# The last stage's entry placed in the last steps of the second attention layer, with two weight sets, and the second batch's rows beside the first products

## The chip, the cores and the metric

One core of one Trainium2 chip runs the whole computation in one launch. The metric is the device time in microseconds (us), the median of several executions. The profiler records one execution; its times are us from the start of its span. The engines are TensorE (PE), VectorE (DVE), ScalarE (ACT), GpSimd (POOL) and SyncE (SP), which only issues transfers here.

## What is computed

A batch of 2 x 512 rows with 512 columns goes through four residual blocks. Each has the form below; only the last two matter here.

```python
x = x + _layernorm(_L1_attn_ref(_layernorm(x), Wq, bq, Wk, bk, Wv, bv, Wo, bo, gq, gk))
x = x + _layernorm(_L1_ffn_ref(_layernorm(x), w1, w3, w2, lora_A1, lora_B1, ...))

def _L1_ffn_ref(x, w1, w3, w2, ...):       # HID = 1376, rank R = 16, SCALING = 2
    h1 = _lora_linear(x, w1, lora_A1, lora_B1)   # x w1' + 2 (x A1') B1'
    h3 = _lora_linear(x, w3, lora_A3, lora_B3)
    return _lora_linear(jax.nn.silu(h1) * h3, w2, lora_A2, lora_B2)
```

The second attention layer has 32 heads of 128, a norm on queries and keys, and a softmax over 512 keys.

## The kernel before

Everything is float32, and each matrix product is made of three TensorE passes over an upper and a lower part of both operands (`product`, L80 to L85; `rest`, L88 to L90, makes a lower part as the full value less the upper one). So every operand needs an upper copy (mostly ScalarE) and a lower one (VectorE or GpSimd).

The 1024 rows are 8 row tiles of 128 (t = 0 to 7), tiles 0 to 3 are batch 0 and 4 to 7 batch 1. The running attention output stands in `acc`, the normed and turned input of a stage in `xT`, and the residual rows in device memory (`kept`).

**Second attention layer** (`paired_attention`). Eight passes over head groups, the middle ones in a hardware loop. A pass has 32 steps (`TILES`), one for each tile of scores; its slots are 8 pairs of head and batch, four steps each. Each engine runs the same list of steps in order, with semaphores between the engines. Work that lags is placed by step: a slot s starts at step 4s; its exchange of the probabilities' 32x32 blocks through the DMA queue (`move`) is issued at 4s + 4, 16 issues, after a write of the inverse row sums; the landed blocks are halved at 4s + 8 and 4s + 9; the product with the values (`pv`) is at 4s + 10; VectorE scales its result one step later (into one buffer, `scaled`), ScalarE and VectorE halve it (`output_hi`, `output_lo`), and output products (`project`) follow. In the last pass the list goes on to step 43 (`END1`): slot 6's product is at step 34, slot 7's at 38, the last output products at 41 and 42, and `add_rows` adds them to `acc`. Batch 0's last output products are at 33 and 34.

**Last stage** (`swiglu_phase`, a block of its own: its instructions start when all engines have left the one before). First an entry, by steps (`norm_steps`, `FIRST`): for each row tile the norm of the attention output (`ATTN`), GpSimd's residual add, the norm of the sum (`FFN_IN`), four transposes on TensorE (`turn`), an upper and a lower part into `xT`. The norm is one statistic, an aggregate and an epsilon on VectorE, a root on GpSimd (`root`), a bias on VectorE (`center`), the scaling on ScalarE (`scaled`). Beside it the weights: HID is 11 sets (o = 0 to 10) of three 128 x 512 pieces (w1, w3, w2). The low-rank factors are folded into each: TensorE makes their product in a `merge` bank (`prepare`), VectorE adds it to the raw piece (`whole`), ScalarE takes the upper part, GpSimd the lower. The factors need the side matrices (`side`) and a small tile for each set. Then n = 0 to 21 steps, o = 0 to 10 for batch 0 and again for batch 1: 24 matmuls for h1 and h3, the gate, and 12 matmuls (`down`) for the step before. In batch 0 set o + 2 is prepared in step o. `FIRST` ends with tile 3 turned, batch 1's norms having begun by then; the turns of tiles 4 to 7 (`LATER`) are in n = 0 and n = 1. SyncE loads everything in the order of its list; both halves of the summed rows are written back to `kept` ahead of set 3's third piece.

## Time and profile before

| | us |
|---|---|
| median of 3 runs | 2255.28 (2251.87 to 2255.32) |
| the profiled execution, its own time | 2258.43 |
| its span | 2256.4 |
| TensorE busy in the span | 2104.3 (93%) |
| VectorE, ScalarE, GpSimd busy | 1673.7, 1350.8, 1220.6 |

The mean granted TensorE clock is 0.969 of full speed. A busy share of a whole span is a mean over stages; for a change at one place the timeline around that place is what counts. In a timeline the bracket at the end of a row tells how long the engine was idle ahead of it and who ended that. A run of equal instructions is one row with its count.

### The profile page before, as it was taken

The numbers are of one execution on the slowest core, as the hardware profiler recorded it, in microseconds if no ns is written. First come the engines' busy times: TensorE is split into PE (matmuls) and PEld (weight loads), VectorE is DVE, ScalarE is ACT, GpSimd is POOL, SyncE is SP. The second block draws the span as 40 slices with busy tenths as digits, with TensorE's granted clock in tenths as the row PEclk, the third lists the DMA queues.
The fourth block names the chain that finished last, engine by engine and source line by source line (L and its number), as shares of the span: only waits on it lengthen the run. The fifth ranks groups of instructions, "written<-read, shape, count | busy, mean of one in ns | idle before, by whom it ended". The sixth has DMA issues, their size and how long they took to land. (4 is left out here: it accounts for less than half of the span.)

```text
span 2256.4 us, 38456 instructions
## 1 busy us (share of the span) xinstructions
PE 2104.3 (93%) x10535; PEld 1776.3 (79%) x10535; DVE 1673.7 (74%) x2974; ACT 1350.8 (60%) x3637; POOL 1220.6 (54%) x983
## 2 busy tenths in 40 slices
PE   6999999999999769999999999999999999847998
PEld 4788888888887657888888888888888888636886
DVE  6778888888788856888788787787887888853422
ACT  5777777777776445666656566565665656533321
POOL 3878778787795544545545454454644445233400
PEclk9999999999999979999999999999999999967999
DMA  2434443434445322434444344443444443443210
GB/s 81 125 104 128 105 116 107 123 92 127 102 109 145 94 80 61 122 102 121 109 113 105 98 117 110 108 112 95 116 114 103 107 105 93 101 121 104 64 52 24
DMA packets 165904, 231.96 MB, mean 103 GB/s; under 512 B 47281, under 2 KB 77137, under 8 KB 165745
## 3 DMA queue, kind: packets, MB, share of 16 engines
q1 hardware_dynamic: 165744, 229.97, 38.4%
q8 instruction: 83, 1.36, 0.3%
q14 instruction: 77, 0.62, 0.1%
HBM read 114.23 MB, written 6.55 MB: 54 GB/s over the span
## 5 line engine op out<-in xcount | busy, mean ns | idle before, releaser
L90 POOL TENSOR_TENSOR l_probsT_lo<-l_moved,l_probsT_hi 128x512 fp32r<-128x512 f32 (+2 forms) x256 | 281.1, 1103 | 314.3 <-ACT l_probsT_hi L620 286.5
L614 ACT ACTIVATE l_probs<-l_score,l_negtop 128x512 f32<-128x512 f32 x256 | 175.7, 686 | 376.1 <-DVE l_negtop L719 375.8
L90 DVE TENSOR_TENSOR l_probsT_lo<-l_moved,l_probsT_hi 128x512 fp32r<-128x512 f32 (+1 forms) x256 | 286.3, 1119 | 33.3 <-ACT l_probsT_hi L620 33.2
L719 DVE TENSOR_REDUCE l_negtop<-l_score 128x1 f32<-128x512 f32 x256 | 176.0, 687 | 91.9 <-PE l_score L85 90.0
L1487 ACT ACTIVATE l_probs<-l_score,l_negtop 128x128 f32<-128x128 f32 (+3 forms) x256 | 134.8, 526 | 178.5 <-DVE l_negtop L1599 177.1
L83 PE MATMUL l_score<-l_kT_lo,l_qT_hi 128*128 128x512 f32 (+3 forms) x512 | 191.5, 374 | 43.5 <-POOL l_qT_lo L90 18.7
L83 PE MATMUL l_out<-l_w_out_lo,l_oT_hi 128*128 128x512 f32 x512 | 209.6, 409 | 5.4 <-DVE l_oT_lo L745 2.8
L1599 DVE CUSTOM_DVE_ANT_0 l_score<-l_score,l_mask 128x128 f32<-128x128 f32 (+3 forms) x256 | 126.2, 493 | 110.0 <-PE l_score L85 108.9
L83 PE MATMUL l_general<-l_w_qk_lo,xT_hi 128*128 128x512 f32 x512 | 201.1, 393 | 1.7 <-PEq L1113 1.7
L85 PE MATMUL l_out<-l_w_out_hi,l_oT_hi 128*128 128x512 f32 x512 | 201.3, 393 | 0.0
L84 PE MATMUL l_out<-l_w_out_hi,l_oT_lo 128*128 128x512 f32 x512 | 201.2, 393 | 0.0
L85 PE MATMUL l_general<-l_w_qk_hi,xT_hi 128*128 128x512 f32 x512 | 201.1, 393 | 0.0
L84 PE MATMUL l_general<-l_w_qk_hi,xT_lo 128*128 128x512 f32 x512 | 201.0, 392 | 0.0
L83 PE MATMUL l_general<-l_probsT_lo,l_v_hi 128*128 128x512 f32 (+3 forms) x512 | 183.5, 358 | 16.1 <-POOL l_probsT_lo L90 10.9
L85 PE MATMUL l_general<-l_probsT_hi,l_v_hi 128*128 128x512 f32 (+3 forms) x512 | 186.1, 363 | 0.0
L84 PE MATMUL l_general<-l_probsT_hi,l_v_lo 128*128 128x512 f32 (+3 forms) x512 | 185.2, 362 | 0.0
L85 PE MATMUL l_score<-l_kT_hi,l_qT_hi 128*128 128x512 f32 (+3 forms) x512 | 183.8, 359 | 0.0
L84 PE MATMUL l_score<-l_kT_hi,l_qT_lo 128*128 128x512 f32 (+3 forms) x512 | 183.7, 359 | 0.0
L734 DVE STREAM_TRANSPOSE l_blocks<-l_probs 128x512 f32<-128x512 f32 x256 | 177.9, 695 | 0.0
L607 ACT ACTIVATE l_squares<-l_y 128x128 f32<-128x128 f32 x512 | 151.9, 299 | 24.5 <-DVE l_y L679 24.5
L90 POOL TENSOR_TENSOR l_w_qk_lo<-l_raw_qk,l_w_qk_hi 128x512 fp32r<-128x512 f32 x60 | 77.7, 1295 | 156.7 <-ACT l_w_qk_hi L584 156.7
L83 PEld LDWEIGHTS l_score<-l_kT_lo,l_qT_hi 128*128 128x128 f32 x512 | 97.3, 190 | 70.6 <-ACT l_probs L1487 20.3
(221 smaller groups left out, 6352.2 us busy)
## 6 DMA issues: line engine op xcount, KB each, us to landing
l_moved<-l_blocks SPq DMA_DIRECT2D x1024, 64.0 KB, 2.0
l_moved<-l_blocks SPq DMA_DIRECT2D x512, 80.0 KB, 2.1
l_inv_all<-inv_rows SPq DMA_DIRECT2D x32, 512.0 KB, 4.4
l_raw_out<-l_wo SPq DMA_DIRECT2D x64, 256.0 KB, 4.5
l_inv_all<-inv_rows SPq DMA_DIRECT2D x64, 256.0 KB, 3.7
ffn_w_lo_words<-f_w SPq DMA_DIRECT2D x33, 256.0 KB, 2.8
l_raw_q<-l_wq SPq DMA_DIRECT2D x32, 256.0 KB, 4.3
l_raw_qk<-l_wq SPq DMA_DIRECT2D x64, 128.0 KB, 2.9
```

What stands on the lines that cost most here:

```text
L83: nc.tensor.matmul(out, left.hi, right.lo, start=first, stop=False, skip_group_check=True)
L84: nc.tensor.matmul(out, left.lo, right.hi, start=False, stop=False, skip_group_check=True)
L85: return nc.tensor.matmul(out, left.hi, right.hi, start=False, stop=last, skip_group_check=True)
L90: return engine.tensor_tensor(out, full, hi.bitcast(F32), ALU.subtract)
L607: last = act.activation(squares[:, h], y[:, b, t, h * HD:(h + 1) * HD], ACT.Square, accum_out=sumsq[:, b, j:j + 1])
L614: act.activation(probs[:, n % NPR], score[n % 2][:], ACT.Exp, bias=negtop[:, n:n + 1], accum_out=total[:, n:n + 1]).then_inc(s_exp, 1)
L719: dve.tensor_reduce(negtop[:, n:n + 1], score[n % 2][:], AXX, ALU.max, negate=True)\
L734: dve.transpose(to, probs[:, n % NPR]).then_inc(s_block, 1)
L1487: act.activation(probs[:, n % NPR, 0:width[t]], score[n % 2][:, 0:width[t]], ACT.Exp, bias=negtop[:, n:n + 1], scale=-1.0, accum_out=total ...
L1599: dve.tensor_tensor_reduce(out=score[n % 2][:, 0:w], in0=score[n % 2][:, 0:w], in1=mask[:, S - w:S], scale=-SCALE, scalar=3.0e38, op0=ALU. ...
```

## The change

A new class `Entry` holds the last stage's entry, its buffers, banks and semaphores. They are laid over the attention's memory: the attention's `y`, `qT`, `kT` and value weights move to the front of its memory, so that what is read latest lies behind what the entry writes. In the attention's last pass each engine gets work in steps 33 to 40, always after what stands in that step already:

- SyncE: the rows of batch 0 and the side matrices at step 22, tiles and pieces of sets 0 and 1 at step 26 (it waits for the slot 7 keys to be out of the transposed rows), the rows of batch 1 at step 33.
- step 33: side matrices and two tiles, upper and lower. Step 34: norms of the attention output of tiles 0 to 3. Step 35: their residual adds. Step 37: the input norms; step 38: their scalings, now into `acc`. Turns on TensorE at 38 (three) and 40; their upper parts at 39 and 40, lower parts at 39 and 40.
- the six merges at steps 34 to 36, the adds at 34, 35 and 37, upper parts at 37 and 38, lower parts at 38 and 39.

In the last stage step n = 0 starts at once. Batch 1's attention norms are at n = 0, the adds on GpSimd at n = 0 and 1, input norms at n = 1 and 2, scalings at 2 and 3, and one tile is turned at the end of each of n = 3 to 6, into a merge bank; sets from 2 on are prepared as before, but the third piece of set 2 at n = 1 ahead of set 3. The summed rows are written back ahead of set 9.

```diff
-END1 = TILES + REST_AT
...
+class Entry:
+    R3 = 96
+    PLACE = [0, 1, 9, 10, 7, 8, 2, 3, 4, 5, 6]
+    NEAR, NEAR2 = 5, 2
+    ROWS_AT, WEIGHTS_AT, MORE_ROWS_AT = 22, 26, 33
+    SIDE_AT, ATTN_AT, ADD_AT = 33, 34, 35
+    MERGE, WHOLE = {34: (0, 1), 35: (2, 3), 36: (4, 5)}, {34: (0, 1), 35: (2, 3), 37: (4, 5)}
+    WHOLE_HI, WHOLE_LO = {37: (0, 1, 2, 3), 38: (4, 5)}, {38: (0, 1, 2, 3), 39: (4, 5)}
+    FFN_IN, SCALE = [TB * (n,) for n in (37, 38)]
+    TURN, UPPER, LOWER = (38, 38, 38, 40), (39, 39, 39, 40), (39, 39, 40, 40)
+    STEPS = range(SIDE_AT, 41)
+    END = TILES + REST_AT
...
+        with ExitStack() as room:
+            self.near, self.near_words = self.tile_and_words(p, room, "ffn_w13_near", [P, self.NEAR, 4, 512])
+            self.tile_raw = p.sb(room, "ffn_tile_raw", [self.R3, 2, 3 * P])
+            self.w2_near, self.w2_near_words = self.tile_and_words(p, room, "ffn_w2_near", [P, self.NEAR2, 2, 512])
+            self.side = p.sb(room, "ffn_side", [self.R3, 3, D], F32R)
+            self.tile = p.sb(room, "ffn_tile", [self.R3, 2, 3 * P], F32R)
+            self.norms = RowNorms(p, room, ctx0, "ffn_norm", 3, half)
+            self.w2_far, self.w2_far_words = self.tile_and_words(p, room, "ffn_w2_far", [P, HT - self.NEAR2, 2, 512])
+            self.far, self.far_words = self.tile_and_words(p, room, "ffn_w13_far", [P, HT - self.NEAR, 4, 512])
+            self.merge, self.h, self.rows = (p.banks(room, n, k) for n, k in (("ffn_merge", 2), ("ffn_h", 2), ("ffn_rows", TB)))
...
+        self.x = self.near_words[:, 2:4].rearrange("p a b s -> p (a b) s")
+        self.side_raw = self.near_words[0:self.R3, 4, 0:3]
...
+    def turned(self, t):
+        return self.rows[t % (TB - 1)] if t < TB else self.merge[(3 * (t + 1) + 3) % 2]
+
...
+    def load_rows(self, sp, b):
+        rows = slice(b * TB, (b + 1) * TB)
+        sp.dma_start(self.x[:, rows], self.kept[:, rows]).then_inc(self.s_x[b], 16)
+
+    def load_side(self, sp):
+        for j, n in enumerate(("f_a1", "f_a3", "f_b2")):
+            sp.dma_start(self.side_raw[:, j], self.a[n]).then_inc(self.s_side, 16)
+
+    def load_weights(self, sp):
+        for o in range(2):
+            sp.dma_start(self.tile_raw[:, o], self.a["f_tile"][o]).then_inc(self.s_tile[o], 16)
+            for j in range(3):
+                sp.dma_start(self.raw(j, o), self.a[("f_w1", "f_w3", "f_w2")[j]][o]).then_inc(self.s_raw[j][o], 16)
+
+    def prepare(self, pe, o, parts=range(3)):
+        side, merge = self.side, self.merge
+        pe.wait_ge(self.s_tile_lo, o + 2)
+        for j in parts:
+            k = 3 * o + j
+            if k >= 2:
+                pe.wait_ge(self.s_whole, k - 1)
+            if j == 0 and TB + 2 <= o < TT + 2:
+                pe.wait_ge(self.s_x_lo, o - 1)
+            low = self.tile[:, o % 2, j * P:(j + 1) * P]
+            if j < 2:
+                for c in range(C):
+                    last = pe.matmul(merge[k % 2][:, c * P:(c + 1) * P], side[:, j, c * P:(c + 1) * P], low,
+                                     start=True, stop=True, skip_group_check=True)
+            else:
+                last = pe.matmul(merge[k % 2][:], low, side[:, j], start=True, stop=True)
+            last.then_inc(self.s_merged, 1)
+
+    def turn(self, pe, t):
+        pe.wait_ge(self.norms.normed[FFN_IN], t + 1)
+        if t == TB - 1:
+            pe.wait_ge(self.s_x_lo, 1)
+        if t >= TB:
+            pe.wait_ge(self.s_whole, 3 * (t + 1) + 2)
+        for c in range(C):
+            last = pe.transpose(self.turned(t)[:, c * P:(c + 1) * P], self.acc[:, t, c * P:(c + 1) * P], self.ident[:])
+        last.then_inc(self.s_turn, 1)
+
+    def tensor(self, pe, n):
+        for t, at in enumerate(self.TURN):
+            if n == at:
+                self.turn(pe, t)
+        for k in self.MERGE.get(n, ()):
+            self.prepare(pe, k // 3, (k % 3,))
+
...
+    def scalar(self, act, n):
+        if n == self.SIDE_AT:
+            act.wait_ge(self.s_side, 48)
+            act.activation(self.side[:], self.side_raw, ACT.Copy, scale=2.0).then_inc(self.s_tile_hi, 1)
+            self.tile_hi(act, 0)
+            self.tile_hi(act, 1)
+        if n == self.ATTN_AT:
+            self.scale_attn(act, range(TB))
+        for t in range(TB):
+            if n == self.SCALE[t]:
+                self.scale(act, t)
+        for t in range(TB):
+            if n == self.UPPER[t]:
+                self.upper(act, t)
+        for k in self.WHOLE_HI.get(n, ()):
+            self.whole_hi(act, k // 3, (k % 3,))
+
+    def scale_attn(self, act, tiles):
+        for t in tiles:
+            self.norms.scaled(act, ATTN1, t, self.acc[:, t], self.acc[:, t])
+
+    def upper(self, act, t):
+        act.wait_ge(self.s_turn, t + 1)
+        act.activation(self.xT.hi[:, :, self.cols(t)], self.by_chunk(self.turned(t)), ACT.Copy).then_inc(self.s_x_hi, 1)
+
+    def scale(self, act, t):
+        self.norms.scaled(act, FFN_IN, t, self.acc[:, t], self.x[:, t])
+
+    def scalar_second(self, act, n):
+
+        if TB <= n < TT:
+            self.upper(act, n)
+        if n == 0:
+            self.scale_attn(act, range(TB, TT))
+        for t in self.pair(n - 2):
+            self.scale(act, t)
+
+    def pair(self, k):
+        return range(TB + 2 * k, TB + 2 * k + 2) if 0 <= k < TB // 2 else []
+
...
+    def sums(self, dve, t):
+        dve.wait_ge(self.s_add, t + 1)
+        self.norms.sums(dve, FFN_IN, t, self.x[:, t])
+        self.norms.spread(dve, (FFN_IN, t))
+
+    def norm_attn(self, dve, tiles):
+        for t in tiles:
+            self.norms.sums(dve, ATTN1, t, self.acc[:, t])
+            self.norms.spread(dve, (ATTN1, t))
+            if t > tiles[0]:
+                self.norms.center(dve, ATTN1, t - 1)
+        self.norms.center(dve, ATTN1, tiles[-1])
+
+    def vector(self, dve, n):
+        if n == self.SIDE_AT:
+            dve.wait_ge(self.s_tile_hi, 1)
+            dve.scalar_tensor_tensor(self.side[32:64], self.side_raw[32:64], 2.0, self.side[32:64].bitcast(F32),
+                                     ALU.mult, ALU.subtract).then_inc(self.s_tile_lo, 1)
+            self.tile_lo(dve, 0)
+            self.tile_lo(dve, 1)
+        if n == self.ATTN_AT:
+            self.norm_attn(dve, range(TB))
+        tiles = [t for t in range(TB) if n == self.FFN_IN[t]]
+        for t in tiles:
+            self.sums(dve, t)
+        for t in tiles:
+            self.norms.center(dve, FFN_IN, t)
+        for t in range(TB):
+            if n == self.LOWER[t]:
+                self.lower(dve, t)
+        for k in self.WHOLE.get(n, ()):
+            self.whole(dve, k // 3, (k % 3,))
+
+    def vector_second(self, dve, n):
+        if TB <= n < TT:
+            self.lower(dve, n)
+        if n == 0:
+            self.norm_attn(dve, range(TB, TT))
+        for t in self.pair(n - 1):
+            self.sums(dve, t)
+        for t in self.pair(n - 2):
+            self.norms.center(dve, FFN_IN, t)
+
+    def add(self, pool, t):
+        pool.wait_ge(self.s_x[t // TB], 16)
+        pool.wait_ge(self.norms.normed[ATTN1], t + 1)
+        pool.tensor_tensor(self.x[:, t], self.x[:, t], self.acc[:, t], ALU.add).then_inc(self.s_add, 1)
+
+    def gpsimd(self, pool, n):
+        if n == self.ATTN_AT:
+            for t in range(TB):
+                self.norms.root(pool, ATTN1, t)
+        if n == self.ADD_AT:
+            for t in range(TB):
+                self.add(pool, t)
+        for t in range(TB):
+            if n == self.FFN_IN[t]:
+                self.norms.root(pool, FFN_IN, t)
+        for k in self.WHOLE_LO.get(n, ()):
+            self.whole_lo(pool, k // 3, (k % 3,))
+
+    def gpsimd_second(self, pool, n):
+        if n == 0:
+            for t in range(TB, TT):
+                self.norms.root(pool, ATTN1, t)
+        for t in self.pair(n):
+            self.add(pool, t)
+        for t in self.pair(n - 1):
+            self.norms.root(pool, FFN_IN, t)
+
+
...
+        y = sb("y", [P, B, TB, 512])
+        qT = split("qT", [P, 2, S])
+        kT = split("kT", [P, 2, S])
+        with ExitStack() as early:
+            raw_v = p.sb(early, "l1_raw_v", [P, C, HW])
+        w_v_lo = sb("w_v_lo", [P, C, HW], F32R)
+        w_v = Split(sb("w_v_hi", [P, C, HW], F32R), w_v_lo)
...
+                    if m.last and n == Entry.ROWS_AT:
+                        sp.wait_ge(s_free, m.done(USES1, ("y", 1, 1, TB - 1)))
+                        entry.load_rows(sp, 0)
+                        entry.load_side(sp)
+                    if m.last and n == Entry.WEIGHTS_AT:
+                        sp.wait_ge(s_free, m.done(USES1, ("tk", SLOTS - 1)))
+                        entry.load_weights(sp)
+                    if m.last and n == Entry.MORE_ROWS_AT:
+                        entry.load_rows(sp, 1)
...
+                    if m.last and n in Entry.STEPS:
+                        if n == Entry.TURN[0]:
+                            pe.wait_ge(s_free, m.done(USES1, ("pv", SLOTS - 2)))
...
+                    if m.last and n in Entry.STEPS:
+                        if n == Entry.ATTN_AT:
+                            dve.wait_ge(s_added, m.done(OUTS1, (1, 0, TB - 1)))
+                        entry.vector(dve, n)
...
@@ -1806,24 +2044,17 @@
                 sp.wait_ge(s_add, (b + 1) * TB)
                 sp.dma_start(batch(kept, b), batch(x, b)).then_inc(s_kept, 16)
 
-            sp.dma_start(batch(x, 0), batch(kept, 0)).then_inc(s_x[0], 16)
-            for o in range(HT):
-                if o == 0:
-                    for j, n in enumerate(("f_a1", "f_a3", "f_b2")):
-                        sp.dma_start(side_raw[:, j], a[n]).then_inc(s_side, 16)
-                if o >= 2:
-                    sp.wait_ge(s_tile_lo, o)
-                sp.dma_start(tile_raw[:, o % 2], a["f_tile"][o]).then_inc(s_tile[o % 2], 16)
-                if o == 1:
-                    sp.dma_start(batch(x, 1), batch(kept, 1)).then_inc(s_x[1], 16)
+            for o in range(2, HT):
+                if o == 9:
+                    sp.wait_ge(norms.normed[FFN_IN], TT)
+                    keep(0)
+                    keep(1)
+                    sp.wait_ge(s_kept, B * 16)
+                sp.wait_ge(entry.s_tile_lo, o)
+                sp.dma_start(entry.tile_raw[:, o % 2], a["f_tile"][o]).then_inc(entry.s_tile[o % 2], 16)
                 for j in range(3):
-                    if o >= 2:
-                        sp.wait_ge(s_whole, 3 * (o - 2) + j + 1)
-                    if j == 2 and o == HT - TT:
...
-                    if n == 0:
-                        prepare(1, (2,))
-                    norm_steps(LATER.get(n, ()))
+                    if n == 1:
+                        entry.prepare(pe, 2, (2,))
                     if b == 0 and o + 2 < HT:
-                        prepare(o + 2, (0, 1))
+                        entry.prepare(pe, o + 2, (0, 1))
                     if n >= 1:
                         down(*divmod(n - 1, HT))
-                    if b == 0 and o + 2 < HT:
-                        prepare(o + 2, (2,))
+                    if b == 0 and 1 <= o < HT - 2:
+                        entry.prepare(pe, o + 2, (2,))
+                        if TB <= n + 1 < TT:
+                            entry.turn(pe, n + 1)
             down(B - 1, HT - 1)
...
                         if o + 2 < HT:
-                            tile_hi(o + 2)
-                        if o + 1 < HT:
-                            whole_hi(o + 1)
-                    norm_steps(LATER.get(n, ()))
+                            entry.tile_hi(act, o + 2)
+                        if 2 <= o + 1 < HT:
+                            entry.whole_hi(act, o + 1)
+                    if n < TT:
+                        entry.scalar_second(act, n)
...
                         if o + 2 < HT:
-                            tile_lo(o + 2)
-                        if o + 1 < HT:
-                            whole(o + 1)
-                    norm_steps(LATER.get(n, ()))
+                            entry.tile_lo(dve, o + 2)
+                        if 2 <= o + 1 < HT:
+                            entry.whole(dve, o + 1)
+                    if n < TT:
+                        entry.vector_second(dve, n)
...
-            norm_steps(FIRST)
             for o in range(HT):
-                if o + 1 < HT:
-                    whole_lo(o + 1)
-                norm_steps(LATER.get(o, ()))
+                if 2 <= o + 1 < HT:
+                    entry.whole_lo(pool, o + 1)
+                entry.gpsimd_second(pool, o)
```

## Rows read from the trace of the kernel before

**Rows 1.** Busy time by stretch (engines as headed, PEclk the granted clock)

```profile
core 0: us, PE busy (x) PEld busy (x) DVE busy (x) ACT busy (x) POOL busy (x), PEclk, DMA share, GB/s
1980.00:2001.50 21.50, 12.10 (x36) 9.09 (x36) 9.51 (x11) 3.63 (x6) 2.95 (x2) 0.76 0.12 28
2001.50:2030.30 28.80, 8.27 (x34) 6.78 (x34) 19.52 (x56) 13.62 (x20) 15.52 (x19) 0.53 0.61 196
2030.30:2072.00 41.70, 27.06 (x96) 22.12 (x96) 16.81 (x37) 16.75 (x26) 15.65 (x17) 0.67 0.31 103
2072.00:2160.00 88.00, 88.00 (x410) 72.17 (x409) 30.23 (x46) 27.83 (x47) 28.88 (x23) 1.00 0.26 83
```

**Rows 2.** Timeline of TensorE (start us, us, engine, line, operation, out<-in)

```profile
2000.19 0.39 PE L85 MATMUL l_out<-l_w_out_hi,l_oT_hi 128*128 128x512 f32 x1
...
2030.30 0.80 PE L83 MATMUL ffn_h<-xT_lo,ffn_w_hi 128*128 128x512 f32 x1
...
2037.89 0.60 PE L1865 MATMUL ffn_rows<-ident,ffn_w_hi_words 128*128 128x128 f32 x4
...
2072.03 0.39 PE L83 MATMUL ffn_h<-xT_lo,ffn_w_hi 128*128 128x512 f32 x1
...
2077.49 1.01 PE L1848 MATMUL ffn_merge<-ffn_tile,ffn_side 96*128 96x128 f32 x8
```

**Rows 3.** Waits of TensorE, 2001 to 2072 (total us, times, longest us)

```profile
PE ffn_rows L1865 <- ACT ffn_w_hi_words L160: 14.8, 4, 5.9
PE ffn_rows L1865 <- DVE ffn_side L1995: 14.4, 1, 14.4
```

**Rows 4.** Timelines of four engines in the attention's last 21 us

```profile
1980.12 1.04 DVE L692 TENSOR_TENSOR l_scaled<-l_general,l_inv_all 128x512 f32<-128x512 f32 x1
...
1983.61 2.19 ACT L620 ACTIVATE l_probsT_hi<-l_moved 128x512 fp32r<-128x512 f32 x4 [1.69 <-DMA l_moved<-l_blocks]
...
1984.31 2.95 POOL L90 TENSOR_TENSOR l_probsT_lo<-l_moved,l_probsT_hi 128x512 fp32r<-128x512 f32 x2 [10.50 <-ACT l_probsT_hi L620]
...
1984.79 3.03 DVE L90 TENSOR_TENSOR l_probsT_lo<-l_moved,l_probsT_hi 128x512 fp32r<-128x512 f32 x2 [2.08 <-ACT l_probsT_hi L620]
...
1985.73 0.77 PE L83 MATMUL l_general<-l_probsT_lo,l_v_hi 128*128 128x512 f32 x1 [6.26 <-POOL l_probsT_lo L90]
...
1990.70 1.05 DVE L692 TENSOR_TENSOR l_scaled<-l_general,l_inv_all 128x512 f32<-128x512 f32 x1 [2.89 <-PE l_general L85]
...
1993.35 0.80 PE L83 MATMUL l_out<-l_w_out_lo,l_oT_hi 128*128 128x512 f32 x1 [2.75 <-DVE l_oT_lo L745]
```

**Rows 5.** Timelines of VectorE, ScalarE and GpSimd in the last stage

```profile
2001.63 0.69 DVE L133 BATCH_NORM_STATS2 ffn_norm_stats<-acc 128x6 f32<-128x512 f32 x1 [0.33 <-PEq L341]
...
2006.41 0.21 DVE L154 TENSOR_SCALAR ffn_norm_bias<-ffn_norm_mean_var,ffn_norm_rstd 128x1 f32<-128x1 f32 x1 [0.30 <-POOL ffn_norm_rstd L148]
...
2079.13 0.69 DVE L90 TENSOR_TENSOR ffn_gT_lo<-acc,ffn_gT_hi 128x512 fp32r<-128x512 f32 x1 [0.70 <-ACT ffn_gT_hi L1966]
...
2080.43 2.11 DVE L1989 TENSOR_TENSOR ffn_w_lo_words<-ffn_merge,ffn_w_lo_words 128x512 f32<-128x512 f32 x3
...
2005.90 2.93 ACT L160 ACTIVATE acc<-acc,ffn_norm_bias,ffn_norm_rstd 128x512 f32<-128x512 f32 x4 [13.39 <-DVE ffn_norm_bias L154]
...
2047.96 1.28 ACT L1958 ACT_TABLE_LOAD   x1
...
2007.63 2.49 POOL L2076 TENSOR_TENSOR ffn_w_lo_words<-ffn_w_lo_words,acc 128x512 f32<-128x512 f32 x2 [1.26 <-DMA ffn_w_lo_words<-x_kept]
```

**Rows 6.** SyncE's issues; times to landing in 2000 to 2030, then in the whole run

```profile
1956.84 0.33 SPq L469 DMA_DIRECT2D inv_rows<-l_inv  x1
1957.44 10.81 SPq L478 DMA_DIRECT2D l_moved<-l_blocks  x16
...
2004.48 1.39 SPq L1826 DMA_DIRECT2D ffn_w_lo_words<-f_w  x3
...
ffn_w_lo_words<-f_w SPq DMA_DIRECT2D x9, 256.0 KB, 6.5
...
ffn_w_lo_words<-f_w SPq DMA_DIRECT2D x33, 256.0 KB, 2.8
```

255 lines of the change are left out of this document (83 added, 172 removed).

## The prediction

> **What bounds the kernel now.** First the stretch table around the border between the second attention layer and the last stage [rows 1]. From 2072.0 on TensorE is busy in every microsecond, up to 2160 at a granted clock of 1.00, so only fewer or faster matmuls would help there, and the change has none. Before it lie three stretches in which TensorE is not the limit: the attention's last 21.5 us (busy 12.1), the stage's entry of 28.8 us (busy 8.3, clock 0.53), and 41.7 us with the first products (busy 27.1, clock 0.67). Then TensorE's own order of time [rows 2]: the last output product of the attention starts at 2000.19, the first product of the last stage at 2030.30, the third step's products at 2072.03; from there each step repeats without a gap. So the border costs 2072.03 - 2000.19 = 71.8 us. The waits say on whom it waits [rows 3]: 14.8 us for normed rows from ScalarE, and 14.4 us for the side matrices, whose transfers are issued only when the attention is over. So the place is a chain of small norms, adds and transfers over five engines. The change starts half of it earlier.
>
> **What the attention's end has room for.** After the last scores TensorE waits for slot 7 (the last head of the last batch): its exchange through the DMA queue, ScalarE's upper part at 1983.61, the lower parts on VectorE and GpSimd, the product at 1985.73, the scaling at 1990.70, the output product at 1993.35 [rows 4]. The added work stands in the same engine queues, ahead of these links. It is free only as long as the link behind it is not due. I walk it in the new program order.
>
> **Loads.** SyncE issues the rows of batch 0, the side matrices and two weight sets earlier. The first go between two exchanges, in a gap. The eight issues of the weight sets cost about 4 us (three take 1.39 us [rows 6], two sets with their two tile loads). They wait for slot 7's keys, as the output-weight fetch behind them waited for its own buffer, and come ahead of that fetch and of slot 6's exchange, which began at 1956.84 and would now begin about 0.8 us later. Slot 7's exchange hangs on slot 6's (16 issues take 10.81 us, and the inverse rows have to land), so it moves by 0.8 us too: its blocks, taken at 1983.61, land at 1984.4. That costs nothing if ScalarE is not ready before, which follows below; without that cover it costs 0.8 us. The two sets are 1.9 MB, and the output weights and slot 6's blocks queue behind them. Weight pieces of this size land after 2.8 us in the median of the run, and after 6.5 us in the backlog of the old entry [rows 6]; so slot 6's exchange could be late by 3.7 us more. Bounds 0 to 4.5 us; I take 0, because slot 7 gets some 4 us of cover from the next paragraph.
>
> **The tail on VectorE, ScalarE and GpSimd.** VectorE's last add for batch 0 ends at 1980.12. Now the four attention norms come next. Old first statistics to the last bias, 2001.63 to 2006.62, is 5.0 us [rows 5]; with the bias steps interleaved 5.3, so 1985.4. Two weight adds, 0.65 us each (the old three in 2.11 [rows 5]): 1986.7. Only then slot 6's scaling, 1980.12 before and now 1986.7. Its ScalarE half ends at 1988.5, and slot 7's upper parts, queued behind it, start there and not at 1983.61. GpSimd does its four roots, then the four row adds (two took 2.49 [rows 5]), 1985.1 to 1990.1, and only then its first part of slot 7: to 1991.6. The product on slot 7 thus starts at 1991.7 instead of 1985.73, 6.0 us late, and ends at 1996.4. VectorE goes on: second lower part to 1992.7, four input norms at 1.0 us each and the last bias 1997.6, two weight adds 1998.9, and only then the scaling of slot 7 (1990.70 before): 8.2 us late. ScalarE has four scalings (2.93 us for four), two weight copies, and then slot 7's output half at 2001.2; VectorE has two lower halves of the turned rows before slot 7's lower output half, which is done at 2004.5. The output product starts at 2004.6 and not at 1993.35. **The attention ends 11.3 us later.** Bounds: 6.0 (the links behind the product hide the rest) and 20 (each of the moved groups, 5.3 + 4.9 + 5.0 + 2.9 + 1.9, lies bare). I take 11.3, the walk. TensorE's own additions (six merges, sixteen turns) run in its gaps.
>
> Here a rule bears on the sum. VectorE's two lower parts of slot 7 took 3.03 us beside GpSimd's two in 2.95 [rows 4]; the same operation with both inputs in SBUF took 0.69 us where GpSimd was idle [rows 5], and GpSimd's adds alone take 1.25 each. The Trainium skill, page "SBUF — State Buffer", section "Who interferes with whom", says that a VectorE instruction with two SBUF inputs contends with a GpSimd instruction that reads SBUF, by an exclusive lock. The rows agree in the sum of both (a pair one after the other would be 0.69 + 1.24 = 1.9, and 1.5 each was measured: most of an exclusion, not all of it). By rows, slot 6's and 7's lower output halves, which now lie beside GpSimd's row adds and weight parts, would take 1.5 us instead of 0.7; that would be 1.6 us more, and it is in the range, not in the sum.
>
> **The new first steps.** From the start of the output product at 1993.35 to the stage's first instruction at 2001.63 it was 8.3 us [rows 4, 5]; so the new stage begins at 2012.9, with batch 0 turned and two weight sets ready. Step 0: TensorE's 24 products, which took 7.4 us with a clock that began low (2030.30 to the one merge ahead of the turns at 2037.89 [rows 2]), end at 2020.3. But VectorE waits for the third tile, issued only at 2012.9 and landed about 2.8 us later [rows 6] (then its copy and lower part: 2016.5), then does the four norms of batch 1 (5.3): 2021.8. ScalarE: the fourth scaling, the table load of 1.28 us [rows 5], the gate: 2024.5. That gate frees step 1's products, 2024.6 to 2032.0 (7.4, cold again). One merge, a weight add (2033.1), two row norms 2.0, product with the gate and its two halves 2.1, the tile and one weight add 1.2: 2038.5. Meanwhile TensorE does the first down products, and its last merge of that step waits for that add. **Step 2's products start at 2038.8 instead of 2072.03: 33.2 us earlier.**
>
> **Later steps.** Of the old border nothing is left behind 2072.03, so the rest moves as a block, with two additions. TensorE had 1.9 us without work before step 2, so its first matmuls can be at 1.2 GHz. At 2.4 GHz one takes 0.23 us (24 from 2072.03 to 2077.49 [rows 2]), at half the clock up to 0.46; four or five of them: 1.0 us. And four turns of batch 1 now stand in steps 3 to 6. Four transposes warm took up to 0.60 us [rows 2], I take 0.4; each turn also waits for the second of VectorE's three weight adds, which in the old rhythm (2080.43 plus 1.4, products ended at 2077.49) comes 0.2 us after TensorE is there [rows 2, 5]. 4 x 0.6 = 2.4 us; bounds 1.6 and 12 (the third rival). The rewrite of the kept rows goes to the ninth tile's load, some 10 us ahead of need: nothing, 3 us if not.
>
> **Sum.** Span 2256.4 - 33.2 + 1.0 + 2.4 = 2226.6. The profiled execution's time was 2258.43, 2.0 above its span: 2228.6. The median of the runs shown, 2255.28, is 3.15 below the profiled execution, so the forecast is 2225.5 us, 1.3% faster. Here 0.2% (4.5 us) is about what a measurement can tell from no change.
>
> **Rivals.**
> *The tail gets longer (0.15).* The moved groups and contended VectorE instructions lie bare ahead of slot 7, and the early weight transfers hold back its exchange. For: five engines' queues are in series there, and the rows show contention of the two engines. Against: ScalarE and GpSimd are busy only 3.6 and 3.0 of 21.5 us [rows 1]. Attention ends 20 us late: 2234.
> *The tail hides more (0.15).* ScalarE's early upper parts and the old slack absorb it; 6 us late, and step 2 at 2033: 2220. Against: VectorE's order puts both scalings behind norms.
> *Batch 1 beside the products stalls TensorE (0.08).* Every step 0 to 6 has waits for ScalarE and VectorE; if the chains at steps 2 to 6 run 2 to 3 us past TensorE's 8.2 us of matmuls, add 12: 2237. Against: in the steady rhythm VectorE is busy 30.2 of 88.0 us [rows 1].
> *The change does not do what it says (0.03).* The early transfers land late enough, or the turns wait so, that the gain is gone: within 5 us of 2255.
> *Slower (0.03).* One mechanism: the gaps in steps 2 to 10 keep TensorE at 1.2 GHz. Each matmul then costs up to 0.23 us more, and a step has 36: 8.3 us a step. From 3.6 such steps on (29.8 / 8.3) the gain is eaten; with seven, 2225.5 + 58 = 2284. For: the clock reads 0.67 where the old gaps are. Against: it reads 1.00 from 2072 to 2160 [rows 1], with the same chains beside the same products.
>
> **How the numbers follow.** Likeliest case 0.56, its own range 2221 to 2230. With both tail cases and most of the stall case the range is 2216 to 2238. Faster by over 0.2%: 0.93 (0.56 + 0.15 + 0.15 + 0.07); same 0.03; slower 0.04.
>
> **What would show it.** In the new profile: slot 7's upper parts start at 1988 and its scaling near 1999; the last attention add ends at 2012.5; TensorE goes from there to the first product within 1 us; the gate of step 0 at 2024; step 2's products at 2039; from step 7 on the same 9.6 us a step. The prediction is wrong if the scaling of slot 7 is not behind the input norms, if step 0's gate waits for a transfer, or if the clock of steps 2 to 6 reads under 0.9.

## Result and profile after

The changed kernel took 2230.35 us (median of four runs, 2227.77 to 2235.79) against 2254.15 for the kernel before (median of four runs: the three behind the median given ahead of the prediction, and one of 2253.02). The ratio is 0.9899, with a 95% interval of 0.9876 to 0.9921. The forecast was 2225.5, with a range of 2216 to 2238: a gain of 29.8 us, where 23.8 was measured. The profiled execution is the slowest of the four: 2235.79 us, its span 2234.0.

The page of the kernel after, its head and two of its rows:

```profile
span 2234.0 us, 38454 instructions
...
PE 2106.3 (94%) x10535; PEld 1774.4 (79%) x10535; DVE 1675.1 (75%) x2974; ACT 1349.5 (60%) x3637; POOL 1221.8 (55%) x983
...
PEclk9999999999999969999999999999999999979999
```

TensorE does the same work in 22.4 us less span. The stretch table of the kernel after, cut where the stages now change (columns as in [rows 1]):

```profile
1980.00:2015.60 35.60, 21.32 (x77) 15.79 (x76) 26.10 (x55) 14.70 (x24) 21.02 (x20) 0.71 0.16 49
2015.60:2043.04 27.44, 19.36 (x78) 15.54 (x79) 14.95 (x34) 10.71 (x17) 12.49 (x13) 0.86 0.32 108
2043.04:2131.00 87.96, 87.45 (x404) 70.36 (x403) 35.32 (x60) 32.50 (x55) 31.37 (x26) 0.99 0.28 91
```

The 28.8 us stretch in which TensorE was busy for 8.3 [rows 1] is gone. In its place the attention's tail is longer and fuller: VectorE is busy for 26.1 of 35.6 us. The timeline of TensorE of the kernel after (last product on values, last output product, first products of steps 0 to 3, then a turn and step 4):

```profile
1994.38 0.77 PE L83 MATMUL l_general<-l_probsT_lo,l_v_hi 128*128 128x512 f32 x1 [2.44 <-POOL l_probsT_lo L90]
...
2006.21 0.79 PE L83 MATMUL l_out<-l_w_out_lo,l_oT_hi 128*128 128x512 f32 x1 [0.22 <-DVE l_oT_lo L1027]
...
2015.60 0.47 PE L83 MATMUL ffn_h<-xT_lo,ffn_w_near 128*128 128x512 f32 x1 [1.20 <-PEq L607]
...
2026.83 0.76 PE L83 MATMUL ffn_h<-xT_lo,ffn_w_near 128*128 128x512 f32 x1 [4.67 <-ACT acc L2124]
...
2042.48 0.77 PE L397 MATMUL ffn_merge<-ffn_side,ffn_tile 96*128 96x512 f32 x1 [2.95 <-DVE ffn_w_far_words L478]
2043.04 0.63 PE L83 MATMUL ffn_h<-xT_lo,ffn_w_far 128*128 128x512 f32 x1
...
2053.88 0.39 PE L83 MATMUL ffn_h<-xT_lo,ffn_w_far 128*128 128x512 f32 x1
...
2063.26 0.47 PE L397 MATMUL ffn_merge<-ffn_side,ffn_tile 96*128 96x512 f32 x1
2063.86 0.63 PE L407 MATMUL ffn_merge<-ident,acc 128*128 128x128 f32 x4
```

The waits of TensorE after the change, 1975 to 2043, the four largest:

```profile
PE ffn_merge L397 <- DVE ffn_w_near_words L478: 5.9, 1, 5.9
PE ffn_h L83 <- ACT acc L2124: 4.7, 1, 4.7
PE ffn_rows L407 <- DVE xT_lo L90: 3.0, 1, 3.0
PE ffn_merge L397 <- DVE ffn_w_far_words L478: 3.0, 1, 3.0
```

The waits of [rows 3], 14.8 and 14.4 us, are gone, and none of the new ones is above 6 us. The same view of the kernel after from 2043 to 2140 has one row, the 3.0 us of L397 that ends at 2042.48: steps 2 to 6 wait for nobody. Step 2's products start at 2043.04 instead of 2072.03, 29.0 us earlier. From there to the end of the span it was 184.4 us and is now 191.0. So 29.0 came in and 6.6 went out again.

### The profile page after: what moved, and what is told of

It is laid out like the page before. It is cut to its first block and busy times, and to the rows that moved or that the text cites. A ratio compares the mean times of both kernels' runs of the same rounds, so it can differ in the third digit from the quotient of the medians.

```text
span 2234.0 us, 38454 instructions
## 1 busy us (share of the span) xinstructions
PE 2106.3 (94%) x10535; PEld 1774.4 (79%) x10535; DVE 1675.1 (75%) x2974; ACT 1349.5 (60%) x3637; POOL 1221.8 (55%) x983
## 5 line engine op out<-in xcount | busy, mean ns | idle before, releaser
L887 ACT ACTIVATE l_squares<-l_y 128x128 f32<-128x128 f32 x512 | 151.9, 299 | 24.6 <-DVE l_y L961 24.6
```

Source lines behind the costliest of these rows:

```text
L887: last = act.activation(squares[:, h], y[:, b, t, h * HD:(h + 1) * HD], ACT.Square, accum_out=sumsq[:, b, j:j + 1])
```

## Experiments

Executions of the same code differ in when the second layer's last score product ends (1958.3 to 1969.9 in the profiled executions of the kernel after and of its variants), and with that in the span. So places in the border are compared by their distance to the start of that last score product. These are differences of timeline rows:

| us after the last score product | output product of slot 7 | first product of the stage | step 2's products |
|---|---|---|---|
| before | 28.2 | 65.2 | 106.9 |
| after | 39.2 | 48.6 | 76.0 |
| again | 39.8 | 49.3 | 76.8 |
| w29 | 39.2 | 48.8 | 76.4 |
| align, align24, align248 | 39.1, 39.3, 39.4 | 48.5, 47.4, 47.3 | 75.9, 73.9, 73.7 |
| late | 28.7 | 60.5 | 87.3 |
| upfront | 39.2 | 69.1 | 88.4 |
| slot_first | 33.1 | 49.1 | 76.9 |
| tile_early | 39.6 | 47.7 | 73.3 |
| te248 | 39.2 | 48.5 | 73.1 |
| best248 | 31.4 | 46.5 | 69.5 |
| shift (a variant of the kernel before) | 27.0 | 64.3 | 106.3 |

The experiments came in three sets, each with its own runs of the kernel before beside it, at 2257.09 (again, align, shift, tile_early), 2254.76 (align24, late, w29, slot_first) and 2257.28 us (the rest). All ratios are to these.

**again.** The changed kernel, unaltered, as the yardstick of the first set.

> The changed kernel unaltered, as the yardstick for the runs beside it. Both theories: a ratio to the kernel before of 0.987 to 0.991 (2227 to 2235 us). In its profile the far weight sets' products (ffn_h) start 0.2335 us apart, those of the near sets 0.228, where the kernel before has 0.2265; if that spacing differs from execution to execution it is chance and not the layout.

Measured 2233.11 us, ratio 0.9890 (0.9875 to 0.9905). It agrees with the first result.

### What the place in the tail is worth

**late.** Every step of the entry moved behind the attention, the early loads and the rows beside the products kept:

```diff
-    SIDE_AT, ATTN_AT, ADD_AT = 33, 34, 35
+    SIDE_AT, ATTN_AT, ADD_AT = 43, 44, 45
...
-    TURN, UPPER, LOWER = (38, 38, 38, 40), (39, 39, 39, 40), (39, 39, 40, 40)
-    STEPS = range(SIDE_AT, 41)
-    END = TILES + REST_AT
+    TURN, UPPER, LOWER = (48, 48, 48, 50), (49, 49, 49, 50), (49, 49, 50, 50)
+    STEPS = range(SIDE_AT, 51)
+    END = 51
```

> The changed kernel with every entry step of the last pass ten steps later, so behind the attention's last output products; the early loads and the spreading of batch 1 stay. My theory (entry and attention's tail are both chains of small links, and each was lengthened by sharing the engines): the attention's last output product starts at about 1994 as before the change, and then batch 0's entry runs bare, 17 to 18 us from the last add to the first product, so the stage starts at about 2019, 3 us later than with the overlap: the overlap itself is worth 3 us and the early loads and the spreading the rest. Rival (the overlap is the gain, as the 14.8 us of waits for normed rows suggest): 10 to 15 us slower than the changed kernel, 2243 us.

Measured 2243.26 us, ratio 0.9944 (0.9925 to 0.9963), against 0.9885 and 0.9888 for the kernels w29 and align24 of the same set (both below). Stretch table of this kernel, the bare entry:

```profile
1999.40:2024.40 25.00, 9.16 (x36) 7.07 (x35) 18.53 (x46) 11.50 (x18) 16.71 (x18) 0.63 0.00 1
```

With the DMA share at 0.00 all weights are there, and the entry of batch 0 still takes 25 us by itself. The attention is done 10.5 us earlier (28.7 against 39.2), but the first product starts 11.9 us later. So the tail hides about half of the entry and pays for the other half by a longer attention. At step 2's products it is 11.3 us (87.3 against 76.0), and in the times about 13 (0.0056 to 0.0059 of 2255 us). The rival was right: I had expected 3.

### What the rows beside the first products are worth

**upfront.** Batch 1's norms, adds and turns all ahead of step 0's products, one tile after the other, batch 0's entry still in the tail:

```diff
+            for t in range(TB, TT):
+                entry.turn(pe, t)
...
-                        if TB <= n + 1 < TT:
-                            entry.turn(pe, n + 1)
...
+            entry.scalar_second(act)
...
-                    if n < TT:
-                        entry.scalar_second(act, n)
```

(VectorE and GpSimd likewise.)

> The changed kernel with one part undone: batch 1's norms, adds, input norms, turns and both parts of xT all stand ahead of step 0's products again, batch 0's entry stays in the attention's tail. Theory (the rows beside the first products are worth a few us, since their place costs other waits): bare, the second batch's chain is about 13 us (four norms 5.3, the last add 1.25 and its pipeline, last input norm 1.0, scalings, turn and two parts some 4), so the first product stands some 61.6 us behind the last score product instead of 48.6; from there steps 0 and 1 no longer wait for the norms (27.4 us to step 2 in the changed kernel, about 20 here), so step 2 is at some 82 us instead of 76.0; and steps 3 to 6 lose the 0.74 us each of the turns. Sum: +6 - 3 = 3 to 4 us slower than the changed kernel, some 2234. Rival 1 (the placement is worth its full chain): step 2 at 89, 10 us slower, some 2240. Rival 2 (worth nothing, VectorE and the clock take it all back): within 1.5 us of the changed kernel.

Measured 2244.02 us, ratio 0.9938 (0.9922 to 0.9953). Its timeline of TensorE between the two stages:

```profile
2013.85 0.39 PE L85 MATMUL l_out<-l_w_out_hi,l_oT_hi 128*128 128x512 f32 x1
2024.42 1.12 PE L403 MATMUL ffn_rows<-ident,acc 128*128 128x128 f32 x4 [10.19 <-ACT acc L160]
2027.40 1.12 PE L403 MATMUL ffn_rows<-ident,acc 128*128 128x128 f32 x4 [1.87 <-ACT acc L160]
2031.34 1.12 PE L403 MATMUL ffn_rows<-ident,acc 128*128 128x128 f32 x4 [2.82 <-ACT acc L160]
2035.28 1.11 PE L403 MATMUL ffn_rows<-ident,acc 128*128 128x128 f32 x4 [2.82 <-ACT acc L160]
```

Bare, the chain of batch 1 puts the first product 20.5 us later (69.1 against 48.6), and not 13: each tile waits for its own root, bias, scaling and turn, and one turn follows the other at 3 to 4 us. From its first statistics at 2015.29 to the first product at 2036.05 VectorE is busy for 10.9 of 20.8 us. The order adds to the waits: VectorE takes the next tile's statistics only behind the lower part of a tile before, which has to be turned first. Step 2 comes 12.4 us later than in the kernel after. From step 2 on 4.1 us come back (186.84 to the end against 190.96), where 3 were expected. That leaves 8.2 us between the two spans. Beside align248 of the same set (below), whose far sets gain 2.2 us, it is 13.6 - 2.2 = 11.4 in the spans and 0.0060 x 2257 - 2.2 = 11.3 in the times. Rival 1 was right. So the rows beside the products are worth 8 to 11 us, and the tail 11 to 13.

No run puts only the loads back to their old place. What they are worth without the other two is not shown. late and upfront each keep them, with one of the two others, and are still 12.6 and 14.0 us faster than the kernel before (ratios 0.9944 and 0.9938).

### The loads

**w29.** The two weight sets loaded behind slot 6's exchange instead of ahead of it:

```diff
-    ROWS_AT, WEIGHTS_AT, MORE_ROWS_AT = 22, 26, 33
+    ROWS_AT, WEIGHTS_AT, MORE_ROWS_AT = 22, 29, 33
```

> The changed kernel with the two early weight sets loaded at step 29, behind slot 6's exchange and the output weights, instead of at 26. Theory A (the 2 us by which the attention's last scores came late is TensorE's clock, not these loads): no change within 1 us, slot 6's exchange starts 0.8 us earlier and nothing follows from it. Rival B (the loads ahead of the output weights and the exchange cost it): ScalarE no longer waits for the output weights, and the time falls by 2 us.

Measured 2230.39 us, ratio 0.9885 (0.9867 to 0.9904). SyncE's queue in the kernel after, and then in this one:

```profile
1957.69 0.34 SPq L736 DMA_DIRECT2D inv_rows<-l_inv  x1
...
1972.40 0.33 SPq L736 DMA_DIRECT2D inv_rows<-l_inv  x1
```

```profile
1957.09 0.33 SPq L736 DMA_DIRECT2D inv_rows<-l_inv  x1
...
1973.45 0.34 SPq L736 DMA_DIRECT2D inv_rows<-l_inv  x1
```

The two writes of inverse sums move by 0.6 us one way and 1.1 us the other, and the border stays (39.2, 48.8, 76.4). Ahead of slot 6's exchange the weight loads cost nothing, as forecast: ScalarE is not ready for slot 7 before 1990. (In both kernels they are early; w29 does not say what it is worth that they are.)

### The order within the tail

**slot_first.** Slot 7's links ahead of batch 0's norms, which are done in pairs, and the second set's lower parts moved into the last stage (these lines are among those left out):

```diff
-    FFN_IN, SCALE = [TB * (n,) for n in (37, 38)]
-    TURN, UPPER, LOWER = (38, 38, 38, 40), (39, 39, 39, 40), (39, 39, 40, 40)
+    NORM, NORM_SCALE, ROOT, ADD = {35: (0, 1), 37: (2, 3)}, {37: (0, 1), 38: (2, 3)}, {35: (0, 1), 38: (2, 3)}, {37: (0, 1), 39: (2, 3)}
...
+    FFN_IN, SCALE = (40, 40, 41, 42), (40, 40, 41, 42)
+    TURN, UPPER, LOWER = (41, 41, 43, 43), (41, 41, 43, 43), (42, 42, 43, 43)
```

> The changed kernel with the tail's order turned round: on every engine the links of slot 6 and 7 stand ahead of the entry's work, the attention norms are split in two pairs (steps 35 and 37), input norms go to steps 40 to 42 and turns to 41 and 43, and the second set's lower parts into the next stage. My theory (the 13 us by which the attention ended later came from program order alone, with idle time left on each engine): slot 7's upper parts start at 1985, its output product at 1996, the stage at 2007 instead of 2015.6, and the time falls by 7 to 9 us. Rival (the entry of batch 0 is the longer chain anyway): what the attention gains the entry loses, the stage starts at 2013 to 2016, within 2 us of the changed kernel.

Measured 2227.74 us, ratio 0.9873 (0.9856 to 0.9890). Timeline of VectorE of this kernel, its last four attention adds and the two input norms between them:

```profile
1995.38 0.68 DVE L1034 TENSOR_TENSOR acc<-l_out,acc 128x512 f32<-128x512 f32 x1
1996.95 0.69 DVE L1034 TENSOR_TENSOR acc<-l_out,acc 128x512 f32<-128x512 f32 x1 [0.90 <-PE l_out L85]
1997.56 0.68 DVE L133 BATCH_NORM_STATS2 ffn_norm_stats<-ffn_w_near_words 128x6 f32<-128x512 f32 x1
...
1999.44 0.68 DVE L1034 TENSOR_TENSOR acc<-l_out,acc 128x512 f32<-128x512 f32 x1
2000.70 0.69 DVE L1034 TENSOR_TENSOR acc<-l_out,acc 128x512 f32<-128x512 f32 x1 [0.57 <-PE l_out L85]
2001.31 0.68 DVE L133 BATCH_NORM_STATS2 ffn_norm_stats<-ffn_w_near_words 128x6 f32<-128x512 f32 x1
```

The attention's output product comes 6.1 us earlier, and the first product of the stage does not (49.1 against 48.6): tile 3's norm now starts at 2001.31, behind the last add. Two chains of nearly equal length share VectorE; shortening one lengthens the other. The span is short here (2226.3) because the last score product was early in this execution (1958.3). The time is not distinguishable from that of w29, the kernel nearest to the changed one in this set (0.9885). In the places the rival was right: what the attention gained the entry lost.

**tile_early.** The third set's small tile is loaded in the tail:

```diff
+                        sp.wait_ge(entry.s_tile_lo, 2)
+                        sp.dma_start(entry.tile_raw[:, 0], a["f_tile"][2]).then_inc(entry.s_tile[0], 16)
...
-                sp.wait_ge(entry.s_tile_lo, o)
-                sp.dma_start(entry.tile_raw[:, o % 2], a["f_tile"][o]).then_inc(entry.s_tile[o % 2], 16)
+                if o > 2:
+                    sp.wait_ge(entry.s_tile_lo, o)
+                    sp.dma_start(entry.tile_raw[:, o % 2], a["f_tile"][o]).then_inc(entry.s_tile[o % 2], 16)
```

> The changed kernel with the third set's small tile loaded in the attention's last steps instead of at the start of the last stage. Theory A (step 0's gate hangs on VectorE's four norms, which stand behind this transfer): VectorE begins the norms within 1 us of the stage's start instead of 3.3 us later, the gate and step 2's products come 2.5 to 3 us earlier, and the time falls by as much. Rival B (the gate hangs on TensorE's 24 products and the table load, or the later steps wait for the weight pieces loaded behind the tile): the gain is under 1 us.

Measured 2228.77 us, ratio 0.9876 (0.9861 to 0.9892). The rows of the kernel after, of ScalarE and VectorE at step 0:

```profile
2017.56 0.53 ACT L421 ACTIVATE ffn_tile<-ffn_tile_raw 96x384 fp32r<-96x384 f32 x1 [10.94 <-DMA ffn_tile_raw<-f_tile]
...
2024.80 1.28 ACT L2124 ACT_TABLE_LOAD   x1
...
2014.43 0.69 DVE L1034 TENSOR_TENSOR acc<-l_out,acc 128x512 f32<-128x512 f32 x1 [0.68 <-PE l_out L85]
2018.11 0.55 DVE L470 TENSOR_TENSOR ffn_tile<-ffn_tile_raw,ffn_tile 32x384 fp32r<-32x384 f32 x1 [2.99 <-ACT ffn_tile L421]
```

and the answering waits of TensorE in tile_early:

```profile
PE ffn_merge L397 <- DVE ffn_w_far_words L478: 3.0, 1, 3.0
PE ffn_h L83 <- ACT acc L2127: 2.6, 1, 2.6
```

TensorE's wait for step 0's gate falls from 4.7 to 2.6 us, the wait for the weight add stays at 3.0. From the first product to step 2 it is 25.65 us (24.6 in te248, below), against 26.35 to 27.6 in the six executions that share all else (after, again, w29, align, align24, align248). So the tile's place is worth about 2 us up to there. The distance to the last score product alone would say 2.7 to 3.5 (73.3 against 76.0 and 76.8), but align24 and align248 reach 73.9 and 73.7 without the early tile: a single execution of each does not resolve 2 us. In the times nothing shows either (0.9876 against 0.9890 for again in the same set, the intervals overlap). By the profile the gain lies between the two forecasts, 2.5 to 3 us and under 1.

### Where the last stage lost 2 us

In the changed kernel the weights for h1 and h3 of five sets (0, 1, 7, 9 and 10, the near ones) lie right behind `xT`, those of the other six (the far ones) behind the small buffers; the w2 pieces have a near part (sets 0 and 1) and a far part too. In the kernel after, the far sets' products for h1 and h3 are spaced 0.233 us from start to start, the near sets' 0.227, and all sets 0.227 before. The groups by line of TensorE, 2142 to 2190, with the mean ns of one as the last figure ahead of the idle time; first the kernel before, then the kernel after:

```profile
L85 PE MATMUL ffn_h<-xT_hi,ffn_w_hi 128*128 128x512 f32 x47 | 18.3, 389 | 0.0
```

```profile
L83 PE MATMUL ffn_h<-xT_lo,ffn_w_far 128*128 128x512 f32 x40 | 15.8, 396 | 0.0
...
L85 PE MATMUL ffn_rows<-ffn_w_near,ffn_gT_hi 128*128 128x512 f32 x8 | 3.2, 396 | 0.0
...
L84 PE MATMUL ffn_h<-xT_hi,ffn_w_near 128*128 128x512 f32 x6 | 2.3, 390 | 0.0
```

**shift.** The kernel before, with 8 unused words ahead of the last stage's weights:

```diff
+        sb("shift", [P, 8])
```

> The kernel before with 8 words of padding ahead of the last stage's weights, so that all weights and the gate's product move by 32 bytes against xT; nothing else changes. Theory A (relative phase): the ffn_h products' spacing rises from 0.2265 to about 0.2335, 24 x 0.007 x 22 steps = 3.7 us, time 2258 us; the ffn_rows products, both of whose operands move, stay at 0.2265. Rival B (place in memory or neighbouring parts): nothing changes, 2254 us.

```profile
L85 PE MATMUL ffn_h<-xT_hi,ffn_w_hi 128*128 128x512 f32 x46 | 18.2, 396 | 0.0
```

Measured 2261.24 us, ratio 1.002 (1.001 to 1.003). One move of 32 bytes, and the products for h1 and h3 take 6 to 7 ns longer (spacing 0.233 us for 0.227); from step 2 to the end it is 187.6 us instead of 184.4. Theory A was right. The down products, both of whose operands moved by these 32 bytes, hardly changed: 0.229 us for 0.228 before. That the place matters is shown, and that it is not the place of one operand alone.

**align** and **align24.** The changed kernel with 8 and with 24 unused words ahead of the far sets:

```diff
+            p.sb(room, "ffn_pad", [P, 8])
...
-        self.size = 6 * HT * 512 + 3 * D + 4 * 3 * P + 3 * TT * 11
+        self.size = 6 * HT * 512 + 3 * D + 4 * 3 * P + 3 * TT * 11 + 8
```

> The changed kernel with 8 words of padding behind the norms' small buffers, so that the far weights and the gate's product begin at a multiple of 64 bytes from the near ones; nothing else changes. Theory A (two operands of a matmul that start at a different phase within 64 bytes cost about 0.007 us a matmul): the far products' spacing falls from 0.2335 to about 0.227, a step in the steady part from 9.70 to 9.56 us, and the span by 2.5 to 3.5 us. Rival B (the spacing comes from where the far sets lie, high in memory, or from upper and lower parts lying side by side): the spacing stays at 0.2335 and the time is that of the changed kernel.

> The changed kernel with 24 words of padding behind the norms' small buffers (8 in the run before, which left the far products at 0.2333). With 24 the far weights and the gate's product begin at a multiple of 128 bytes from xT, as everything does in the kernel before. Theory A, second form (what counts is the phase within 128 bytes): far spacing 0.227, a steady step 9.56 instead of 9.70 us, from step 2's products to the span's end 188.5 us instead of 191.2. Rival B (place in memory, upper and lower part side by side): 0.2333 and 191.2 us as before.

Measured 2230.68 us, ratio 0.9882 (0.9867 to 0.9897), and 2229.80, ratio 0.9888 (0.9870 to 0.9906). The far sets in align24:

```profile
L85 PE MATMUL ffn_h<-xT_hi,ffn_w_far 128*128 128x512 f32 x38 | 15.0, 395 | 0.0
```

In align they take 395 ns too, at a spacing of 0.233 us in both. Both theories, a period of 64 bytes and one of 128, fell.

**align248.** The same with 248 words, which puts every far piece and the gate's product at a multiple of 512 words (2 KB) from `xT`, as in the kernel before. (The two near w2 pieces stay 256 words off such a multiple, in all these variants.)

> The changed kernel with 248 unused words (992 bytes) ahead of the far weight sets, so that all their pieces stand at a multiple of 512 words from xT, as all sets do in the kernel before (pads of 8 and 24 words left the spacing of their products at 0.233 us). Theory (what counts is the place of the weights against xT or the start of memory with a period of up to 2 KB): the far sets' h1 and h3 products are spaced 0.227 us instead of 0.233, 24 of them in 5.22 us instead of 5.37, and the stage from step 2 on is some 2.5 us shorter; median some 2227.5. Rival (what counts is that the far sets lie high in memory, or another thing that the pad leaves): spacing stays at 0.233, and the time is that of the changed kernel.

```profile
L85 PE MATMUL ffn_h<-xT_hi,ffn_w_far 128*128 128x512 f32 x40 | 15.6, 389 | 0.0
...
L85 PE MATMUL ffn_rows<-ffn_w_near,ffn_gT_hi 128*128 128x512 f32 x7 | 2.7, 389 | 0.0
```

Measured 2230.26 us, ratio 0.9878 (0.9863 to 0.9892). The spacing is back at 0.227 us, far sets as near ones. From step 3's products to the end of the span it is 177.9 us, against 180.1 in the kernel after: 2.2 us. In the times 2.2 us don't show apart from the kernel after (0.9878, and 0.9890 for again; the intervals overlap). So it is not that the sets lie high in memory.

The down products tell what the place counts against. In the kernel after, the far w2 pieces and the gate's product both stand 1056 bytes behind a multiple of 2 KB from `xT`, so with a distance of 0 between them modulo 2 KB, and their products are spaced 0.228 us as before the change. The near w2 pieces stand 32 bytes off the gate's product, and theirs are spaced 0.233 (396 ns). In align248 this distance is 1024 bytes, and they are back at 0.227 (389 ns). By the sizes of the kernel's buffers, modulo 2 KB, the distances between the two operands were: slow at 32, 64, 128, 1056, 1088 and 1152 bytes, fast at 0 and 1024. So it is the distance between the two operands of a matmul that counts, and if it does so periodically, the period is 256, 512 or 1024 bytes. Which of them is open, and why is not shown.

### Together

**te248** is tile_early and align248 in one; **best248** is those two and slot_first.

> Both: the third set's tile loaded in the attention's tail (which made step 2 come 2.9 us earlier against the last score), and the pad of 248 words. Theory of the placement period: the two gains add, 2.9 + 2.5 us less than the changed kernel, some 2225. Rival (the pad does nothing): as the kernel with the early tile alone, some 2228.

> The two above and slot 7's links ahead of batch 0's norms, which are split in pairs. Alone that order brought the attention's end 6.1 us forward and the first product of the last stage not at all. With the tile early, VectorE starts batch 1's norms as soon as batch 0's lower parts are done. Theory (the entry of batch 0 is the longer chain in the tail): same time as the kernel with early tile and pad, within 1.5 us. Rival (the two together free what each alone could not): 3 us and more less than that kernel.

Measured 2229.86 us, ratio 0.9864 (0.9846 to 0.9882), and 2227.14, ratio 0.9855 (0.9836 to 0.9874). In te248 the tile's gain up to step 2 was given back at once: TensorE's granted clock is low there, and step 2 took 12.0 us (2040.06 to 2052.10), against 10.8 in the kernel after and 9.6 in align248. The theory's 2225 us for te248 was missed by 4.9. In best248 step 2's products come 3.5 us earlier than in te248 and 6.5 earlier than in the kernel after; the rival was right in the profile, and the median is 2.7 us lower, which the intervals don't separate. best248 is the lowest of all. Against the kernel after and again, from other sets, the medians are 3.2 and 6.0 us lower and the ratios 0.0044 and 0.0035, and its interval ends at 0.9874 where theirs begin at 0.9876 and 0.9875. So it beats the kernel before, and probably the one after, by something between 3 and 10 us. That is said with care: it is the lowest of several variants, and measured in another set.

## Why the prediction was right

The direction, the mechanism and the time (4.9 us off in the median) held. In the profiled execution, which the sum was made for, 7.4 us were missed: 2226.6 against 2234.0.

The signs that the prediction named came in the order it gave, at times 1.6 to 4.2 us late: slot 7's scaling at 2000.80 stands behind the input norms (last bias at 1999.47), the last add ends at 2015.12 and the first product starts 0.5 us behind it, the gate is at 2026.09, step 2 at 2043.04, and step 7 takes 9.64 us. One sign of being wrong is half there: the gate hangs on a transfer, through the norms. ScalarE waited until 2017.56 for the third tile, VectorE's norms stand behind its lower part, and the gate behind their scalings. But that wait was a term of the sum, and tile_early shows about 2 us for it up to step 2.

By its steps:

- **Loads: right.** Slot 6's inverse row sums left 0.85 us later (1957.69 for 1956.84; 0.8 forecast), and w29 shows that this costs nothing.
- **Last score product, not forecast: 1.9 us.** It came at 1967.0 instead of 1965.1. In w29 it came at 1965.4, in again, with the same code as after, at 1968.3: no more than executions differ.
- **Tail: right, +11.0 us for +11.3.** Against the last score product slot 7's output product moved by 39.2 - 28.2. The rows of VectorE, ScalarE and GpSimd of the kernel after answer to the walk:

```profile
1982.15 0.69 DVE L133 BATCH_NORM_STATS2 ffn_norm_stats<-acc 128x6 f32<-128x512 f32 x1
...
1988.49 1.08 DVE L974 TENSOR_TENSOR l_scaled<-l_general,l_inv_all 128x512 f32<-128x512 f32 x1
...
1991.40 3.39 DVE L90 TENSOR_TENSOR l_probsT_lo<-l_moved,l_probsT_hi 128x512 fp32r<-128x512 f32 x2
...
2000.80 1.10 DVE L974 TENSOR_TENSOR l_scaled<-l_general,l_inv_all 128x512 f32<-128x512 f32 x1
...
2005.27 0.88 DVE L1027 SCALAR_TENSOR_TENSOR l_oT_lo<-l_scaled,l_b_v,l_oT_hi 128x512 fp32r<-128x512 f32 x1
...
1990.23 2.17 ACT L900 ACTIVATE l_probsT_hi<-l_moved 128x512 fp32r<-128x512 f32 x4
...
1987.10 5.46 POOL L535 TENSOR_TENSOR ffn_w_near_words<-ffn_w_near_words,acc 128x512 f32<-128x512 f32 x4
...
1992.53 3.40 POOL L90 TENSOR_TENSOR l_probsT_lo<-l_moved,l_probsT_hi 128x512 fp32r<-128x512 f32 x2
```

  Slot 6's scaling was forecast for 1986.7, slot 7's upper parts for 1988.5, its scaling for 1998.9: each came 1.7 to 1.9 us later, which is the last score's delay and no more. The intervals between them hold within 0.1 to 0.2 us; each had been worked out from program order and durations of equal instructions. The product on slot 7 (1994.38, forecast 1991.7) came another 0.8 us late, as GpSimd's row adds and both engines' lower parts took longer than in the old place; it cost nothing, since the scaling behind it waited for VectorE's norms anyway.
- **Contention, kept out of the sum: half right.** The prediction's rows would have made slot 7's lower output half and slot 6's 1.5 us each. They took 0.88 and 0.73. The rule of the Trainium skill (page "SBUF — State Buffer", section "Who interferes with whom") is an exclusive lock; in these two rows the trace does not bear it out. GpSimd's row adds beside the second took 1.37 us each instead of 1.25, and the two lower parts of slot 7 3.39 us for 3.03. In slot_first the same lower output half took 1.44 us beside GpSimd's adds, so the price does occur, and what decides it is not shown. In the kernel after it fell elsewhere: the lower half of step 1's gate took 1.71 us beside GpSimd's adds, and 0.69 in the old place [rows 5]:

```profile
2039.32 1.71 DVE L90 TENSOR_TENSOR ffn_gT_lo<-acc,ffn_gT_hi 128x512 fp32r<-128x512 f32 x1 [0.70 <-ACT ffn_gT_hi L2132]
...
2037.96 2.52 POOL L535 TENSOR_TENSOR ffn_w_near_words<-ffn_w_near_words,acc 128x512 f32<-128x512 f32 x2
```

- **Output product to first product: 9.4 us for 8.3.** The 24 output products took 7.8 us from first to last start and not 6.8, at a granted clock of 0.68 (2006.2 to 2014.4) instead of 0.77 (1993.35 to 2000.5); the price was copied from the old tail.
- **First product to step 2: 27.4 us for 25.9.** The gate was at 2026.09, 1.6 us after its forecast, of which the later first product had given 2.7; so the tile and the norms took 1.1 us less than thought. From the gate on it was 16.95 us for 14.3: 1.0 for the contended lower half, 0.6 for the later start of step 1's products (2026.83, 0.7 us behind the gate's first instruction), 0.5 for these products themselves (7.9 for 7.4), and 0.5 in small pieces.
- **From step 2 on: 6.6 us for 3.4.** Step 2 itself lost 1.3 to its cold clock (1.0 forecast). The four turns cost 0.7 to 0.8 each, some 3.1 (2.4 forecast): in the row at 2063.86 the transposes come 0.6 us behind the merge, and the next step's product 0.4 behind them. The remaining 2.2 us are the place of the far sets, and of the near w2 pieces, in memory. No step of the prediction had it, since I priced a matmul by its shape alone. The four runs shift and align to align248 showed that term.

What went against me (1.9 + 1.1 + 1.5 + 3.2, less 0.3 of the tail) is 7.4 us. That the median was nearer is luck, with no reason in the argument: the profiled execution lay 5.4 us above its median, and the one before 3.15 above the median it was compared with. Of the rivals, the clock one (slower) did not come: the clock reads 0.92 from 2044 to 2054 and 1.00 from there.

My explanation of the gain was the weaker part. I held the tail's place for worth 3 us before late, and batch 1's rows for 3 to 4 before upfront; they measured 11 to 13 and 8 to 11. Both times I had costed a chain over several engines by little more than the work of its longest engine. Bare, the chains took 25.0 and 20.8 us, with VectorE busy for 18.5 and 10.9 of it; the rest is waits from one engine to the next.
